# The combine stage of a mixture of experts: gate scaling on ScalarE and one VectorE add for five tiles

## The chip, the cores and the metric

The kernel runs on one core of one Trainium2 chip. The metric is the device time of one execution in microseconds (us); lower is better.

## What is computed

Two layers on 3125 nodes with 256 features. The first layer is a graph attention layer and a mixture of eight experts with the two best experts per node; the second is a plain graph sum and an attention over slices. The change lies between the two layers, where the experts' results are combined and the next layer norm and product are made:

```python
out = jnp.einsum('ne,nec->nc', gates, y)        # two gates per node are not zero
x = x + _L0_ffn_ref(...)                        # x += gate0 * y_first + gate1 * y_second
x = x + _L1_gnn_ref(_layernorm(x), L1_gnn_W, ...)  # starts with layernorm(x) @ W.T
```

## The kernel before, in words

The 3125 nodes are 25 tiles of 125 rows (`NT`), taken in 5 groups of 5 tiles (`GROUPS`, `TB`). The residual `k.res` stays in SBUF for the whole kernel. The stages are blocks with a barrier between them; the engines' programs are written out by hand, each engine works its own queue in that order, and semaphores join them. No planner moves anything.

`experts_phase` ends with the combine stage. Every result of an expert has been scattered to the DRAM table `y_tab`; SyncE waits for all of it (L1922 and around) and then loads, group by group, the first results and the second results of the five tiles into `ys`, which lies in the room of the expert weights (the trace calls it `weights`). Semaphores `ys_in[g]` and `seconds_in[g]` say that they have landed.

- **VectorE**, per group g: five `scalar_tensor_tensor` (L2188) make `res += gate0 * first`; then `invert(g-1)`, the reciprocal of the roots of the group before (L2182, waits for ScalarE's root); then five more (L2194) make `res += gate1 * second`, each raising `rows_made` by one; then five `bn_stats` (L2197) and four small operations (L2199 to L2202) for the variance, the last of which raises `deviations`.
- **TensorE**, per tile t: waits for `rows_made`, turns the tile into PSUM with two transposes (L2052), and then multiplies tile t-1 with the centred weight matrix (L2059, two products in float32). So the product of a group's last tile stands behind the transposes of the next group's first tile.
- **ScalarE**, per group: five copies of the turned tiles to SBUF (L2119), the square root of the variances (L2121), a wait for VectorE's reciprocal (`scaled`), and five scalings of the products by `rstd` into `xn` (L2125; the trace calls `xn` `e_x`), each waiting for its product.
- **SyncE** stores each scaled group to the DRAM table `xn_tab`. When all is stored the block ends, and `sum_phase` begins to gather rows of `xn_tab` with GpSimd (L1204).

The order on ScalarE that the change touches:

```python
for g in range(GROUPS):
    for t in tiles: ... nc.scalar.copy(yt[...], YT[...])        # L2119
    act.wait_ge(deviations, g + 1)
    nc.scalar.activation(k.rstd[...], spread[...], ACT.Sqrt, ...)   # L2121
    act.wait_ge(scaled, g + 1)
    for t in tiles: ... nc.scalar.activation(xn[:, t, :], XT[...], ACT.Identity, scale=k.rstd[...])  # L2125
```

Of the kernel before, what the change touches and what calls it, by code (L numbers as in the profile page):

```python
# [21 lines left out]
ALU = mybir.AluOpType  # L22
ACT = mybir.ActivationFunctionType
# [6 lines left out]
TB = 5  # L30
# [33 lines left out]
class Kernel:  # L64
# [10 lines left out]
    def sem(self, name):  # L75
        s = self.nc.semaphore(name)
        if self.opened is None:
            return self.ctx.enter_context(s)
        self.opened.append(self.layer.enter_context(s))
        return self.opened[-1]  # L80
# [973 lines left out]
class Prep:  # L1054
# [60 lines left out]
    def share(self, dve, t):  # L1115

        k = self.k
        k.steps["dve"](dve, k.nc.vector.scalar_tensor_tensor(out=k.res[:, t, :], in0=self.bias[:, :], scalar=self.part[:, t:t + 1], in1=k.res[:, t, :], op0=ALU.mult, op1=ALU.add))
# [745 lines left out]
def experts_phase(k):  # L1864
# [3 lines left out]
    nc = k.nc  # L1868
    ctx = ExitStack()
    X = XAHEAD  # L1870
    with ctx:
        sb = lambda n, s, d=F32: k.sb(f"e_{n}", s, d, ctx)
        sem = lambda n: k.sem(f"e_{n}")
# [12 lines left out]
        ys = k.weights[0:P, :, :].rearrange("p a w -> p (a w)")[:, 0:2 * NT * C].bitcast(F32).rearrange("p (j t c) -> p j t c", j=2, t=NT)  # L1886
        xn = x_more[0:P, 0:NT, :]
        GROUPS = NT // TB
# [3 lines left out]
        gw_mean, eps = sb("gw_mean", [128, 2]), sb("eps", [P, 1])  # L1892
        gap, spread = sb("gap", [P, NT]), sb("spread", [P, NT])
        gw_in, gw_centred, gw_turned, gw_ready = (sem(n) for n in ("gw_in", "gw_centred", "gw_turned", "gw_ready"))
        rows_made, y_turned, yt_kept, multiplied, xt_scaled = (sem(n) for n in ("rows_made", "y_turned", "yt_kept", "multiplied", "xt_scaled"))
        y_rows = k.y_tab.rearrange("(j t p) c -> p j t c", t=NT, p=P)
        deviations, roots, scaled, out_done = (sem(n) for n in ("deviations", "roots", "scaled", "out_done"))
        ys_in, seconds_in = [sem(f"ys_in{g}") for g in range(GROUPS)], [k.gather_sem(f"e_seconds_in{g}") for g in range(GROUPS)]
# [50 lines left out]
        def steps(start, item, finish):  # L1949


            start()
            for i in range(1, NI):
                item(i)
            finish()

        @block.tensor
        def _(pe):
# [86 lines left out]
            pe.wait_ge(y_kept, NI + 2)  # L2045
            for t in range(NT + 1):
                if t < NT:
                    pe.wait_ge(rows_made, t + 1)
                    if t >= XR:
                        pe.wait_ge(yt_kept, t - XR + 1)  # L2050
                    for c in range(2):
                        m = nc.tensor.transpose(YT[t % XR][:, c * P:(c + 1) * P], k.res[:, t, c * 128:(c + 1) * 128], k.ident[0:P, 0:P])  # L2052
                    m.then_inc(y_turned, 1)
                if t:
                    pe.wait_ge(yt_kept, t)
                    if t > len(XT):
                        pe.wait_ge(xt_scaled, t - len(XT))
                    for c in range(2):
                        m = nc.tensor.matmul(XT[(t - 1) % len(XT)], yt[:, (t - 1) % XR, c, :], gwt[:, c, :], start=(c == 0), stop=(c == 1))  # L2059
                    m.then_inc(multiplied, 1)  # L2060

        @block.scalar
        def _(act):
            act.sem_inc(y_kept, 2)

            def keep_x(i, s):
                act.wait_ge(x_turned, i + 1)
                act.wait_ge(up, 2 * i)
                nc.scalar.copy(xt[s][0][:, :, :].rearrange("p a m -> p (a m)"), TURN[:, 0:2 * M]).then_inc(x_high, 1)

            def silu(n, a):
                act.wait_ge(up, n + 3)
                act.wait_ge(h_made, n + 1)
                nc.scalar.activation(gated[a][:, 0:HH[a]], UP[a][:, 0:HH[a]], ACT.Silu).then_inc(silued, 1)  # L2074

            def keep_h(n, a):
                act.wait_ge(h_turned, n + 3)
                act.wait_ge(down, n + 1)
                nc.scalar.copy(ht[a][0][:, 0:2, :].rearrange("p b m -> p (b m)"), TH[:, 0:2 * M])
                nc.scalar.copy(ht[a][0][0:TAIL[a], 2, :], TH[0:TAIL[a], 2 * M:3 * M]).then_inc(h_high, 1)  # L2080

            def keep_y(i, s):
                act.wait_ge(down, 2 * i + 4)
                nc.scalar.copy(k.x_row(i), DOWN[s][:, 0:C]).then_inc(y_kept, 1)  # L2084

            def start():
                act.wait_ge(k.staged_in, 16)
                for raw, high, low in firsts:
                    nc.scalar.copy(high, raw).then_inc(first_high, 1)
                act.wait_ge(x_turned, 1)  # L2090
                nc.scalar.copy(xt[0][0][:, :, :].rearrange("p a m -> p (a m)"), TURN[:, 0:2 * M]).then_inc(x_high, 1)
                silu(0, 0)
                silu(1, 1)
                keep_x(1, 1)
                keep_h(0, 0)

            def item(i):
                silu(2 * i, 0)
                keep_h(2 * i - 1, 1)
                silu(2 * i + 1, 1)  # L2100
                if i < NI - 1:
                    keep_x(i + 1, (i + 1) % 2)
                keep_h(2 * i, 0)
                keep_y(i - 1, (i - 1) % 2)

            def finish():
                keep_h(2 * NI - 1, 1)
                keep_y(NI - 1, 1)

            steps(start, item, finish)  # L2110
            act.wait_ge(gw_turned, 1)
            nc.scalar.copy(gwt.rearrange("p a c -> p (a c)"), YT[0][:, 0:2 * C]).then_inc(gw_ready, 1)
            for g in range(GROUPS):
                tiles = range(g * TB, (g + 1) * TB)
                for t in tiles:
                    act.wait_ge(y_turned, t + 1)
                    if t >= XR:
                        act.wait_ge(multiplied, t - XR + 1)
                    nc.scalar.copy(yt[:, t % XR, :, :].rearrange("p a n -> p (a n)"), YT[t % XR][:, 0:2 * P]).then_inc(yt_kept, 1)  # L2119
                act.wait_ge(deviations, g + 1)  # L2120
                nc.scalar.activation(k.rstd[:, g * TB:(g + 1) * TB], spread[:, g * TB:(g + 1) * TB], ACT.Sqrt, bias=eps[:, 0:1], scale=1.0 / C).then_inc(roots, 1)  # L2121
                act.wait_ge(scaled, g + 1)
                for t in tiles:
                    act.wait_ge(multiplied, t + 1)
                    nc.scalar.activation(xn[:, t, :], XT[t % len(XT)], ACT.Identity, scale=k.rstd[:, t:t + 1]).then_inc(xt_scaled, 1)  # L2125

        @block.vector
        def _(dve):
            v = nc.vector
# [49 lines left out]
            def invert(g):  # L2179
                rstd = k.rstd[:, g * TB:(g + 1) * TB]  # L2180
                dve.wait_ge(roots, g + 1)
                v.reciprocal(rstd, rstd).then_inc(scaled, 1)  # L2182

            for g in range(GROUPS):
                tiles = slice(g * TB, (g + 1) * TB)
                dve.wait_ge(ys_in[g], 32)
                for t in range(g * TB, (g + 1) * TB):
                    m = v.scalar_tensor_tensor(out=k.res[:, t, :], in0=ys[:, 0, t, :], scalar=k.gate[:, 0, t:t + 1], in1=k.res[:, t, :], op0=ALU.mult, op1=ALU.add)  # L2188
                me(dve, m)
                if g:  # L2190
                    invert(g - 1)
                dve.wait_ge(seconds_in[g], 32)
                for t in range(g * TB, (g + 1) * TB):
                    v.scalar_tensor_tensor(out=k.res[:, t, :], in0=ys[:, 1, t, :], scalar=k.gate[:, 1, t:t + 1], in1=k.res[:, t, :], op0=ALU.mult, op1=ALU.add).then_inc(rows_made, 1)  # L2194
                dve.wait_ge(rows_made, (g + 1) * TB)
                for t in range(g * TB, (g + 1) * TB):
                    m = v.bn_stats(k.stats[:, t, :], k.res[:, t, :])  # L2197
                me(dve, m)
                v.tensor_tensor(spread[:, tiles], k.stats[:, tiles, 2], k.stats[:, tiles, 5], ALU.add)  # L2199
                me(dve, v.tensor_tensor(gap[:, tiles], k.stats[:, tiles, 1], k.stats[:, tiles, 4], ALU.subtract))  # L2200
                me(dve, v.scalar_tensor_tensor(out=gap[:, tiles], in0=gap[:, tiles], scalar=0.25 * C, in1=gap[:, tiles], op0=ALU.mult, op1=ALU.mult))
                v.tensor_tensor(spread[:, tiles], spread[:, tiles], gap[:, tiles], ALU.add).then_inc(deviations, 1)  # L2202
# [384 lines left out]
```

## Time and profile before

| | |
|---|---|
| median of 3 runs | 1933.1 us (1930.58 to 1934.11) |
| the profiled execution's own time | 1931.59 us |
| its span, first to last instruction | 1929.3 us |
| mean granted TensorE clock | 0.839 of full speed |
| TensorE, VectorE, ScalarE, GpSimd busy | 72%, 46%, 31%, 56% of the span |
| combine stage, first load issued to last product scaled | about 1180 to 1230 us |

Busy shares are means over stages with different limits. A timeline row gives start, length, engine, line, operation and, in brackets, how long the engine stood idle before it and what ended the wait. "x5" is five instructions merged into one row. PE is TensorE, DVE VectorE, ACT ScalarE, POOL GpSimd, SPq the queue of SyncE. [...]

### The profile page before, as it was taken

What the parts mean: (1) busy time and instruction counts of PE and PEld (TensorE: products, weight loads), DVE (VectorE), ACT (ScalarE), POOL (GpSimd) and SP (SyncE); (2) the same over time, 40 slices, a digit from 0 to 9 for tenths busy, and PEclk for the clock granted to TensorE, in tenths of its full rate; (3) what the DMA queues carried; (4) which work ended last, traced back from release to release, by engine and by line L of the source; (5) the groups of instructions that cost most, each with busy time, mean ns of one, the idle gap of its engine ahead of it and who ended that gap; (6) DMA issues with size and microseconds to landing.
All of it is one profiled execution on the core that took longest, in us unless ns stands there. A gap on an engine that the chain in (4) does not pass through costs nothing. (4 is left out here: it accounts for less than half of the span.)

```text
span 1929.3 us, 24683 instructions
## 1 busy us (share of the span) xinstructions
PE 1397.2 (72%) x7091; PEld 1166.9 (60%) x7091; DVE 878.9 (46%) x1858; ACT 594.9 (31%) x1305; POOL 1076.6 (56%) x1064
## 2 busy tenths in 40 slices
PE   6646666656665772899999996566666666668998
PEld 5535454445444762899999995444454444446787
DVE  6445544443444578333333334555333333336943
ACT  4144333333333233333333332322222222222310
POOL 1577777777773501783222570277777777763520
PEclk9857877877777685999999998787777888878999
DMA  6577989888886604432111125633333333330002
GB/s 164 129 226 249 301 282 307 269 275 295 287 277 207 147 1 124 147 87 92 46 47 47 44 93 106 178 104 104 106 105 104 106 105 105 106 88 1 0 1 67
DMA packets 156099, 266.53 MB, mean 138 GB/s; under 512 B 26388, under 2 KB 119331, under 8 KB 154953
## 3 DMA queue, kind: packets, MB, share of 16 engines
q1 hardware_dynamic: 106742, 138.90, 23.3%
q0 software_dynamic: 45424, 122.33, 21.0%
q10 hardware_dynamic: 3811, 3.78, 0.8%
q8 instruction: 64, 1.05, 0.2%
q14 instruction: 58, 0.48, 0.1%
HBM read 167.96 MB, written 97.93 MB: 138 GB/s over the span
## 5 line engine op out<-in xcount | busy, mean ns | idle before, releaser
L1204 POOL DMA_INDIRECT sum_rows<-xn_tab,src_e x391 | 373.2, 954 | 174.8 <-issue 118.8
L1229 PE MATMUL bank<-sum_held,sum_hot 128*125 128x256 f32 x976 | 309.3, 481 | 189.4 <-ACT sum_held L1239 188.1
L817 POOL DMA_INDIRECT gat_rows<-xh_tab,src_e x363 | 343.5, 946 | 114.7 <-issue 109.4
L1229 PEld LDWEIGHTS bank<-sum_held,sum_hot 128*125 128x125 f32 x976 | 225.3, 239 | 269.5 <-issue 175.1
L890 PE MATMUL bank<-gat_rows,gat_same 128*128 128x264 f32 x784 | 259.7, 477 | 126.1 <-issue 126.1
L890 PEld LDWEIGHTS bank<-gat_rows,gat_same 128*128 128x128 f32 x784 | 173.7, 240 | 165.2 <-issue 132.5
L1239 ACT COPY sum_held<-sum_rows 128x1024 f32 x122 | 127.5, 1045 | 373.3 <-SPq L1195 336.0
L1981 PE MATMUL bank<-weights,e_xthigh 128*128 x896 | 219.0, 328 | 10.0 <-DVE e_xtlow L2136 5.4
L934 ACT COPY gat_outs<-bank 128x528 f32<-128x528 f32 x196 | 117.3, 598 | 282.9 <-PE bank L890 282.4
L2141 DVE TENSOR_TENSOR e_h<-e_gated,bank 128x342 f32<-128x342 f32 x112 | 57.1, 510 | 263.5 <-ACT e_gated L2074 263.5
L1261 DVE SCALAR_TENSOR_TENSOR res<-bank,prep_inv,res 125x256 f32 x122 | 58.9, 483 | 235.0 <-PE bank L1229 228.0
L1981 PEld LDWEIGHTS bank<-weights,e_xthigh 128*128 128x128 f32 x896 | 152.6, 190 | 19.4 <-issue 19.3
L1981 PE MATMUL bank<-weights,e_xtlow 128*128 x448 | 143.9, 321 | 0.0
L2002 PE MATMUL bank<-weights,e_hthigh 128*128 (+2 forms) x672 | 134.6, 296 | 0.3 <-DVE e_htlow L2146 0.3
L2074 ACT ACTIVATE e_gated<-bank 128x342 f32<-128x342 f32 x112 | 51.0, 455 | 239.8 <-PE bank L1981 239.8
L1860 POOL CAST weights<-staged 128x4264 fp32r<-128x4264 f32 x7 | 26.3, 3751 | 151.9 <-SPq L1919 142.3
L854 DVE TENSOR_TENSOR gat_rows<-gat_rows,bank 128x1792 f32<-128x1792 f32 x56 | 110.3, 2009 | 0.8 <-ACT bank L926 0.8
L2002 PEld LDWEIGHTS bank<-weights,e_hthigh 128*128 128x128 f32 (+2 forms) x672 | 103.4, 191 | 0.5 <-issue 0.5
L2002 PE MATMUL bank<-weights,e_htlow 128*128 x336 | 94.4, 281 | 0.0
L1981 PEld LDWEIGHTS bank<-weights,e_xtlow 128*128 128x128 f32 x448 | 85.2, 190 | 0.0
L838 DVE TENSOR_TENSOR gat_logit<-gat_rows,adst_e 128x112 f32<-128x112 f32 x28 | 7.7, 277 | 164.2 <-DMA gat_rows<-xh_tab,src_e 164.2
L1946 POOL DMA_INDIRECT y_tab<-e_x,slot_row x52 | 50.9, 979 | 34.4 <-ACT e_x L2084 20.6
(537 smaller groups left out, 2500.5 us busy)
## 6 DMA issues: line engine op xcount, KB each, us to landing
parts<-gat_outs SPq DMA_DIRECT2D x27, 1904.0 KB, 8.0
staged<-w_tab SPq DMA_DIRECT2D x8, 2132.0 KB, 8.8
w_tab<-w_stage SPq DMA_DIRECT2D x16, 682.0 KB, 10.5
w_raw<-in_L_ffn_w_dram SPq DMA_DIRECT2D x16, 640.0 KB
gat_rows<-xh_tab,src_e POOLq DMA_INDIRECT x391, 4.6
sum_rows<-xn_tab,src_e POOLq DMA_INDIRECT x391, 2.8
w_tab<-w_stage SPq DMA_DIRECT2D x8, 768.0 KB, 10.6
weights<-y_tab SPq DMA_DIRECT2D x10, 600.0 KB
```

Of the source, the lines that this page charges most:

```text
L817: pool.indirect_dma_start(out=rows[b % R][:, t, :], out_offset=None, in_=k.xh_tab, in_offset=bass.IndirectOffsetOnAxis(ap=k.src_e[:, b * S ...
L854: v.tensor_tensor(f, f, weight[b % 2][:, t0 * H:t1 * H].rearrange("p (t h a) -> p t h a", h=H, a=1).to_broadcast([EP, SB // 2, H, D]), ALU ...
L890: m = nc.tensor.matmul(k.pairs[duo % DUOS][:, t % 2, 0:sums_w], same[b % 2][:, t, :], rows[b % R][:, t, 0:sums_w], start=True, stop=True)
L934: nc.scalar.copy(outs[b % 2][:, t:t + 2, 0:sums_w], k.pairs[duo % DUOS][:, :, 0:sums_w]).then_inc(taken, 1)
L1204: pool.indirect_dma_start(out=rows[:, at // IP % (RING * GPAIRS), at % IP, :], out_offset=None, in_=k.xn_tab, in_offset=bass.IndirectOffse ...
L1229: m = nc.tensor.matmul(k.ps[s][0:P, 0:C], hot[g % 2][:, s, c, :], held[:, s, c, :], start=(c == 0), stop=(c == IP - 1))
L1239: nc.scalar.copy(held_pair(n), pair).then_inc(staged, 1)
L1261: v.scalar_tensor_tensor(out=into, in0=k.ps[s][0:P, 0:C], scalar=prep.inv[:, bass.ds(node, 1)], in1=into, op0=ALU.mult, op1=ALU.add).then_ ...
L1981: last = nc.tensor.matmul(bank[:, 0:HH[a]], xt[s][px][:, c, :], part(slot, up_at(m, pw, c) + HB[a], 128, HH[a]), start=(n == 0), stop=(n = ...
L2002: m = nc.tensor.matmul(DOWN[s][:, 0:C], ht[a][ph][0:rows, b, :], part(slot, down_at(pw, 3 * a + b), rows, C), start=(a == 0 and n == 0), s ...
L2074: nc.scalar.activation(gated[a][:, 0:HH[a]], UP[a][:, 0:HH[a]], ACT.Silu).then_inc(silued, 1)
L2141: v.tensor_tensor(h[a][:, 0:HH[a]], gated[a][:, 0:HH[a]], GATE[a][:, 0:HH[a]], ALU.mult).then_inc(h_made, 1)
```

## The change

ScalarE gets a helper `share(g)`: it waits for the second results of group g and scales its five tiles by their gates from `ys` into `xn` (whose room is written again only later, by L2125). It is called once for group 0 ahead of the loop, and for group g+1 between the copies and the square root of group g. VectorE's five `scalar_tensor_tensor` per group become one `tensor_tensor` over 5 x 256 columns, which waits for the five scaled tiles; `rows_made` now counts groups, and TensorE waits for the whole group ahead of its first tile.

```diff
-                    pe.wait_ge(rows_made, t + 1)
+                    pe.wait_ge(rows_made, t // TB + 1)
...
+            def share(g):
+                act.wait_ge(seconds_in[g], 32)
+                for t in range(g * TB, (g + 1) * TB):
+                    nc.scalar.activation(xn[:, t, :], ys[:, 1, t, :], ACT.Identity, scale=k.gate[:, 1, t:t + 1]).then_inc(shared, 1)
+
+            share(0)
             for g in range(GROUPS):
...
                     nc.scalar.copy(yt[:, t % XR, :, :].rearrange("p a n -> p (a n)"), YT[t % XR][:, 0:2 * P]).then_inc(yt_kept, 1)
+                if g < GROUPS - 1:
+                    share(g + 1)
                 act.wait_ge(deviations, g + 1)
...
-                dve.wait_ge(seconds_in[g], 32)
-                for t in range(g * TB, (g + 1) * TB):
-                    v.scalar_tensor_tensor(out=k.res[:, t, :], in0=ys[:, 1, t, :], scalar=k.gate[:, 1, t:t + 1], in1=k.res[:, t, :], op0=ALU.mult, op1=ALU.add).then_inc(rows_made, 1)
-                dve.wait_ge(rows_made, (g + 1) * TB)
+                dve.wait_ge(shared, (g + 1) * TB)
+                v.tensor_tensor(k.res[:, tiles, :], xn[:, tiles, :], k.res[:, tiles, :], ALU.add).then_inc(rows_made, 1)
+                dve.wait_ge(rows_made, g + 1)
```

## Rows read from the trace of the kernel before

**Rows 1.** Windows; columns: us, busy and count per engine, PEclk, DMA, GB/s.
```profile
1190.00:1197.00 7.00, 6.20 (x19) 4.76 (x20) 6.35 (x19) 1.47 (x4) 0.00 (x0) 0.53 1.07 197
1214.00:1221.00 7.00, 5.89 (x30) 4.55 (x30) 6.48 (x21) 3.93 (x12) 0.00 (x0) 1.00 0.75 238
```

**Rows 2.** Timeline of VectorE, from one reciprocal to the next.
```profile
1213.67 0.19 DVE L2182 RECIPROCAL rstd<-rstd 125x5 f32<-125x5 f32 x1 [0.38 <-ACT rstd L2121]
1213.77 2.03 DVE L2194 SCALAR_TENSOR_TENSOR res<-weights,gate,res 125x256 f32<-125x256 f32 x5
...
1220.60 0.19 DVE L2182 RECIPROCAL rstd<-rstd 125x5 f32<-125x5 f32 x1 [0.38 <-ACT rstd L2121]
```

**Rows 3.** Timeline of ScalarE, same stretch.
```profile
1213.89 1.57 ACT L2125 ACTIVATE e_x<-bank,rstd 125x256 f32<-125x256 f32 x4 [0.32 <-DVE rstd L2182]
...
1215.98 0.63 ACT L2119 COPY staged<-bank 128x250 f32<-128x250 f32 x2
...
1219.94 0.37 ACT L2119 COPY staged<-bank 128x250 f32<-128x250 f32 x1 [0.71 <-PE bank L2052]
1220.20 0.30 ACT L2121 ACTIVATE rstd<-e_spread,e_eps 125x5 f32<-125x5 f32 x1
```

**Rows 4.** Timeline of TensorE, same stretch.
```profile
1214.27 0.43 PE L2052 MATMUL bank<-ident,res 125*128 125x125 f32 x2 [0.44 <-DVE res L2194]
...
1217.36 0.38 PE L2052 MATMUL bank<-ident,res 125*128 125x125 f32 x2
...
1218.44 0.38 PE L2052 MATMUL bank<-ident,res 125*128 125x125 f32 x2
...
1221.21 0.44 PE L2052 MATMUL bank<-ident,res 125*128 125x125 f32 x2 [0.44 <-DVE res L2194]
```

**Rows 5.** Timeline, the start of the stage's first group.
```profile
1190.12 2.07 DVE L2194 SCALAR_TENSOR_TENSOR res<-weights,gate,res 125x256 f32<-125x256 f32 x5 [1.42 <-DMA weights<-y_tab]
...
1190.76 1.07 PE L2052 MATMUL bank<-ident,res 125*128 125x125 f32 x4 [13.15 <-DVE res L2194]
...
1193.73 0.62 PE L2052 MATMUL bank<-ident,res 125*128 125x125 f32 x2
...
1195.85 0.62 PE L2052 MATMUL bank<-ident,res 125*128 125x125 f32 x2
```

**Rows 6.** Groups by line and shape, whole kernel; columns: busy us, mean ns, idle before.
```profile
L1587 DVE TENSOR_TENSOR join_main<-join_main,join_wt 125x1280 f32<-125x1280 f32 x5 | 7.5, 1492 | 0.2
...
L1730 ACT ACTIVATE r_xn<-res,r_shift,rstd 125x256 f32<-125x256 f32 x25 | 12.4, 586 | 0.0
...
L2112 ACT COPY staged<-bank 128x512 f32<-128x512 f32 x1 | 0.6, 585 | 0.3 <-PE bank L2042 0.3
...
L2399 ACT ACTIVATE t_logit<-t_logit 125x512 f32<-125x512 f32 x25 | 15.9, 636 | 2.7 <-POOL t_logit L2262 2.7
```

**Rows 7.** Timeline, the end of the stage.
```profile
1227.70 1.93 ACT L2125 ACTIVATE e_x<-bank,rstd 125x256 f32<-125x256 f32 x5 [0.26 <-DVE rstd L2182]
...
1230.01 0.40 SPq L140 DMA_DIRECT2D xn_tab<-e_x  x1
...
1235.08 1.00 POOL L1204 DMA_INDIRECT sum_rows<-xn_tab,src_e  x1 [55.94 <-POOLq L1871]
```

**Rows 8.** Timeline of TensorE in the next stage, two bursts after a wait.
```profile
1308.73 3.25 PE L1229 MATMUL bank<-sum_held,sum_hot 128*125 128x256 f32 x8 [2.74 <-ACT sum_held L1239]
...
1318.91 7.12 PE L1229 MATMUL bank<-sum_held,sum_hot 128*125 128x256 f32 x24 [3.22 <-ACT sum_held L1239]
```

**Rows 9.** Windows around those two bursts; columns as in Rows 1.
```profile
1309.00:1312.00 3.00, 2.99 (x8) 1.84 (x6) 1.36 (x2) 0.00 (x0) 2.27 (x3) 0.54 0.38 113
...
1319.00:1320.00 1.00, 1.00 (x4) 0.85 (x5) 0.00 (x0) 1.00 (x1) 0.69 (x2) 0.74 0.44 131
1320.00:1322.00 2.00, 2.00 (x6) 1.54 (x6) 0.00 (x0) 0.00 (x0) 1.70 (x2) 0.50 0.44 121
1322.00:1323.00 1.00, 1.00 (x4) 0.82 (x3) 0.67 (x2) 0.12 (x1) 0.69 (x2) 0.55 0.26 78
```

More of the change, by code:

```diff
@@ L1894, in experts_phase @@
         gw_in, gw_centred, gw_turned, gw_ready = (sem(n) for n in ("gw_in", "gw_centred", "gw_turned", "gw_ready"))
-        rows_made, y_turned, yt_kept, multiplied, xt_scaled = (sem(n) for n in ("rows_made", "y_turned", "yt_kept", "multiplied", "xt_scaled"))
+        rows_made, y_turned, yt_kept, multiplied, xt_scaled, shared = (sem(n) for n in ("rows_made", "y_turned", "yt_kept", "multiplied", "xt_scaled", "shared"))
         y_rows = k.y_tab.rearrange("(j t p) c -> p j t c", t=NT, p=P)
```

## The prediction

> **What bounds the kernel now.** I read the windows first, to see where in the span the change lies and which engines are full there, then one timeline of a single group on three engines, and last the start and the end of the stage. In a window of the combine stage VectorE is busy 6.48 of 7.00 us, TensorE 5.89 and ScalarE 3.93 [rows 1]. The obvious reading is that VectorE is nearly full and ScalarE has room for five more operations. The timeline says otherwise. A group takes from one reciprocal to the next, 1213.67 to 1220.60, 6.93 us, and each time VectorE has waited for ScalarE's square root just before its reciprocal [rows 2]. The root itself starts right behind the group's fifth copy (1219.94, then 1220.20), and that copy had waited for TensorE's transposes [rows 3]. The transposes follow each other every 1.08 us (1217.36 to 1218.44), and the burst opens 0.50 us after VectorE's first L2194 starts (1213.77 to 1214.27) [rows 2, 4]. So the group's cycle is a ring: reciprocal, first gated add, TensorE's five tiles, fifth copy, root, reciprocal. Only what lies in that ring sets the time. ScalarE's idle time lies inside the ring, ahead of its copies, and is of no use to an instruction queued behind the last copy. Nothing after the stage takes a delay back: the last products are scaled from 1227.70 on, the last store is issued at 1230.01, and GpSimd, idle for 55.94 us, starts the next stage's gathers at 1235.08 [rows 7].
>
> **What it adds, in the ring.** Three things get longer.
>
> *The price of one gate scaling on ScalarE.* The trace has no activation of 125x256 from SBUF with one pointer operand. Below it lies L2125, the same with a PSUM source: four take 1.57 us and five 1.93, so one more costs 0.36 [rows 3, 7]. Above it lies L1730, SBUF to SBUF with two pointer operands: 12.4 us for 25, 0.50 each [rows 6]. An SBUF source without pointers costs 0.05 more than a PSUM copy of the same 512 columns (636 against 585 ns) [rows 6]. I take 0.36 + 0.05 = 0.41, the row that differs in the source alone plus that difference. One alone then lasts 1.57 - 3 x 0.36 + 0.05 = 0.54, and five 4 x 0.41 + 0.54 = 2.18 us.
>
> [...]
>
> *The start.* Before, L2194 starts at 1190.12 when the second results land, and TensorE at 1190.76 [rows 5]. After, ScalarE starts at that landing and takes 2.18; then VectorE adds the five tiles in one operation. Its price is L1587's, the same operation on 125x1280: 1.49 us [rows 6]. TensorE, which now waits for the whole group, started 0.50 after the first add when warm; it will start about 1.51 after the big one does. So the start is late by 2.18 + 1.51 - 0.50 = 3.2 us.
>
> *The four later groups.* Behind the same reciprocal the five adds take 2.03 [rows 2] and the one 1.49, so VectorE saves 0.54 a group. But TensorE could start after the first of five and must now wait for the one: 1.51 against 0.50, 1.01 us later. That is 4 x 1.01 = 4.0 us. The fifth scaling of the group before waits for a product queued behind those transposes, so it is late by the same step, not by more.
>
> *The shares in the loop.* Group g+1's five scalings sit between the fifth copy and the root of group g, four times: 4 x 5 x 0.41 = 8.2 us. The root's own input has been ready long before, so the whole of it is added. The new wait there, for the second results of the next group, costs nothing: at 1213.77 L2194 found them landed [rows 2], and ScalarE asks for the same ones only after the copies of the group before, which the terms above move to about 1222. If a load were late there, the root, the five scalings and the next copies behind it would all be late with it.
>
> Free are: VectorE's new wait for `shared` (the scalings precede the root that releases the reciprocal ahead of it), the five statistics (they end long before the root is due), and the stores, which follow the last scaling and come late by the same sum. SyncE's loads are queued ahead of its stores as before, GpSimd has nothing in this stage. Up to here: 3.2 + 4.0 + 8.2 = 15.4 us.
>
> *The clock.* This is the term that the instruction list doesn't show. Between two bursts TensorE now stands idle for 0.44 us [rows 4]; with 1.01 and 5 x 0.41 added it will be 3.5 us, four times. In the next stage, bursts after a wait of 2.74 and 3.22 us run into a lower level: the mean granted clock is 0.54 in the three us from 1309, and after 1318.91 it goes 0.74, 0.50, 0.55 [rows 8, 9]. [...] At that level a tile takes 2.12 us (1193.73 to 1195.85) instead of 1.08 [rows 4, 5], so 3.4 us at the low level cost 1.7 us of work. Some of it falls where TensorE waits for ScalarE's copies anyway; I take 1.6, four times, 6.4 us. The lower bound is nothing, if the clock holds. The upper is a burst like the first group's, which started cold: a mean of 0.53 over 1190 to 1197 [rows 1, 5] puts the rise at 1196.6, 5.8 us after its start, 2.9 us of work lost; 4 x 2.9 = 11.6.
>
> **The sum** is 15.4 + 6.4 = 21.8 us. Against the profiled execution's own 1931.59 (its span of 1929.3 and 2.3 around it) that gives 1953.4; the median of the runs shown, 1933.1, is 1.5 above that execution and gives 1954.9. I forecast 1955.
>
> **The rivals.**
> - *The clock holds* in the longer waits. For it: in this stage it reads 1.00 throughout a warm window [rows 1], and a wait falls nearer to 3.3 us if the scalings cost 0.36. Against it: 2.74 us was enough elsewhere [rows 8, 9]. It gives 15.4 alone, 1947 to 1949. Chance 0.13.
> - *Whole bursts run at the low level*, because a burst this short is over before the clock rises. Each burst then loses 5 x 1.04 = 5.2 us: 15.4 + 20.8 = 36.2, 1968 to 1969. For it: the first group needed 5.8 us; against it: 3.4 us sufficed at 1319. Chance 0.08.
> - *Not slower: VectorE is the bound*. Place: VectorE's queue between two reciprocals, 6.48 busy in 7.00 [rows 1], 0.38 idle. If that queue set the cycle, and ScalarE's scalings ran in its waits before the copies, the 0.54 saved would come off five times, -2.7 us, 1930.4. It decides if the root is ready before VectorE comes to the reciprocal; every row of a reciprocal shows VectorE waiting for it [rows 2], and the added scalings stand ahead of that root in a queue worked in order. Chance 0.03.
> - *The change doesn't do what it says*: another table load on ScalarE for these activations, 25 small ones and no gain. L2125 is the same function and ran behind the root with nothing in between [rows 3, 7], so I give it no time and 0.02 for this and all else.
>
> **How the numbers follow.** The forecast's own case has 0.74. Its bounds: scalings of 0.36 or 0.50 move the sum by -1.2 or +2.1; the clock's term by -6.4 or +5.2. The low end takes in the holding clock with cheap scalings: 1954.9 - 6.4 - 1.2 = 1947.3, and 1945.8 from the profiled execution's own time: 1946. The high end takes the forecast with cold bursts like the first group's and a little of the dear scalings: 1954.9 + 5.2 + 0.9 = 1961. Left out are the rival of whole cold bursts, the not-slower one and the rest, 0.13. A measurement of this kernel tells about 0.2%, 3.9 us, from no change. Of the cases only the third lies within that, so slower has 0.95, no change 0.04 and faster 0.01.
>
> **What would show it.** In the profile after: five activations from `weights` into `e_x` between the fifth copy and each of the first four roots, 2.0 to 2.2 us together; one add of 1.49 us; the first transposes at 3.2 us after their old distance from the landing; reciprocals 10 to 12 us apart instead of 6.93, the last gap about 8 to 10; waits of some 3.5 us ahead of L2052; a granted clock that falls to 0.50 once per group. Wrong would be: reciprocals under 8 us apart, scalings that overlap the copies' waits, or a next stage that starts at its old time. If the clock stays at 1.00 in the stage, the first rival holds; if it stays at 0.50, the second.

## The result, and the profile after

The changed kernel takes 1957.09 us (median of 4 runs, 1955.07 to 1959.39) against 1933.61 of the kernel before in the same comparison: ratio 1.0129, 95% interval 1.0114 to 1.0144, 23.5 us slower. The forecast was 1955.

The profiled execution of after took 1959.39 us. Where the time lies is seen best by the stage alone, from ScalarE's last copy of an expert's result to the first gather of the next stage. The two timelines give 58.06 us before and 81.58 after, 23.5 more; so all of the difference lies here (the experts' stage ahead of it ended 4.3 us later in this one execution). First the row of before that opens the stage (it ends at 1235.08, [rows 7]):

```profile
1177.02 0.37 ACT L2084 COPY e_x<-bank 128x256 f32<-128x256 f32 x1 [2.24 <-PE bank L2002]
```

then the two of after:

```profile
1181.31 0.37 ACT L2084 COPY e_x<-bank 128x256 f32<-128x256 f32 x1 [2.24 <-PE bank L2002]
...
1262.89 1.00 POOL L1204 DMA_INDIRECT sum_rows<-xn_tab,src_e  x1 [79.46 <-POOLq L1871]
```

The timeline of VectorE after, the counterpart of [rows 2]:

```profile
1209.29 0.19 DVE L2190 RECIPROCAL rstd<-rstd 125x5 f32<-125x5 f32 x1 [6.64 <-ACT rstd L2129]
1209.40 1.45 DVE L2201 TENSOR_TENSOR res<-e_x,res 125x1280 f32<-125x1280 f32 x1
...
1222.02 0.19 DVE L2190 RECIPROCAL rstd<-rstd 125x5 f32<-125x5 f32 x1 [6.75 <-ACT rstd L2129]
...
1233.15 0.19 DVE L2190 RECIPROCAL rstd<-rstd 125x5 f32<-125x5 f32 x1 [5.15 <-ACT rstd L2129]
...
1245.90 0.19 DVE L2190 RECIPROCAL rstd<-rstd 125x5 f32<-125x5 f32 x1 [6.77 <-ACT rstd L2129]
...
1255.29 0.19 DVE L2190 RECIPROCAL rstd<-rstd 125x5 f32<-125x5 f32 x1 [5.07 <-ACT rstd L2129]
```

The distances are 12.73, 11.13, 12.75 and 9.39 us instead of four times 6.9. VectorE's work is shorter (1.45 for the add), and what it gained it spends waiting for the root, 5 to 7 us a group instead of 0.38. The timeline of ScalarE after, the end of a group (compare [rows 3]), shows what stands ahead of the root now:

```profile
1194.53 2.10 ACT L2116 ACTIVATE e_x<-weights,gate 125x256 f32<-125x256 f32 x5 [12.02 <-DMA weights<-y_tab]
...
1219.37 0.37 ACT L2125 COPY staged<-bank 128x250 f32<-128x250 f32 x1 [0.71 <-PE bank L2052]
1219.63 2.10 ACT L2116 ACTIVATE e_x<-weights,gate 125x256 f32<-125x256 f32 x5
1221.64 0.28 ACT L2129 ACTIVATE rstd<-e_spread,e_eps 125x5 f32<-125x5 f32 x1
```

The timeline of TensorE after: the first transposes of the five bursts, with the waits ahead of them in brackets (compare [rows 4, 5]):

```profile
1198.38 1.07 PE L2052 MATMUL bank<-ident,res 125*128 125x125 f32 x4 [16.48 <-DVE res L2201]
...
1210.90 0.68 PE L2052 MATMUL bank<-ident,res 125*128 125x125 f32 x2 [4.86 <-DVE res L2201]
...
1223.63 0.43 PE L2052 MATMUL bank<-ident,res 125*128 125x125 f32 x2 [3.44 <-DVE res L2201]
...
1234.76 0.68 PE L2052 MATMUL bank<-ident,res 125*128 125x125 f32 x2 [3.44 <-DVE res L2201]
...
1247.83 0.43 PE L2052 MATMUL bank<-ident,res 125*128 125x125 f32 x2 [3.76 <-DVE res L2201]
```

The windows of after over groups 1 to 4, two to a group (columns as in [rows 1]; PEclk is the third entry from the end):

```profile
1210.00:1216.00 6.00, 4.69 (x13) 3.33 (x14) 5.13 (x15) 2.08 (x6) 0.00 (x0) 0.57 1.07 204
1216.00:1222.00 6.00, 4.20 (x19) 3.23 (x17) 0.00 (x0) 3.29 (x9) 0.00 (x0) 0.86 0.56 164
1223.00:1227.00 4.00, 2.96 (x10) 2.13 (x11) 3.86 (x13) 1.81 (x6) 0.00 (x0) 0.68 0.07 19
1227.00:1233.00 6.00, 4.32 (x21) 3.19 (x20) 1.00 (x3) 3.24 (x9) 0.00 (x0) 0.93 0.36 94
1234.00:1240.00 6.00, 4.83 (x13) 3.49 (x14) 4.99 (x15) 1.94 (x6) 0.00 (x0) 0.56 0.23 49
1240.00:1246.00 6.00, 4.07 (x19) 3.09 (x17) 0.10 (x1) 3.29 (x9) 0.00 (x0) 0.87 0.20 61
1247.00:1251.00 4.00, 2.76 (x9) 1.96 (x10) 3.09 (x10) 1.69 (x5) 0.00 (x0) 0.67 0.00 0
1251.00:1256.00 5.00, 5.00 (x25) 4.19 (x25) 0.19 (x1) 1.79 (x6) 0.00 (x0) 0.92 0.49 128
```

PEclk, the clock granted to TensorE as a share of full speed, was 1.00 throughout a group before [rows 1]; now it falls in each of the four bursts. Taken in windows of 1 us it reads 0.50 in all six from 1211 to 1217 (group 1) and in both from 1249 to 1251 (group 4).

### The profile page after: what moved, and what is told of

The parts are those of the page before. It is cut to its first block and busy times, and to the rows that moved or that the text cites. A ratio compares the mean times of both kernels' runs of the same rounds, so it can differ in the third digit from the quotient of the medians.

```text
span 1957.4 us, 24689 instructions
## 1 busy us (share of the span) xinstructions
PE 1406.4 (72%) x7091; PEld 1174.0 (60%) x7091; DVE 875.1 (45%) x1838; ACT 604.7 (31%) x1330; POOL 1075.1 (55%) x1064
## 5 line engine op out<-in xcount | busy, mean ns | idle before, releaser
L1247 DVE TENSOR_TENSOR sum_hot<-bank,walk_local 128x2000 f32<-128x2000 f32 x31 | 69.0, 2226 | 2.6 <-DMA prep_bias<-in_L_gnn_b_dram 2.6
```

Of the source, the lines that this page charges most:

```text
L1247: v.tensor_tensor(hot[g % 2][:, :, :, :], lane.rearrange("p (a b n) -> p a b n", a=1, b=1).to_broadcast([EP, IB, IP, P]), w.local[:, g * I ...
```

## The experiments

Ratios are to the kernel before, with 95% intervals. "Distances" are those between the five reciprocals, "stage" the length from ScalarE's last copy of an expert's result to the first gather, as above; both come from the one profiled execution of each run.

**1 and 2: hold the clock.** TensorE multiplies the unit matrix while it waits; the second run has 13 products instead of 18.

```diff
-                    pe.wait_ge(rows_made, t // TB + 1)
                     if t >= XR:
                         pe.wait_ge(yt_kept, t - XR + 1)
+                    if t and t % TB == 0:
+                        for _ in range(18):
+                            nc.tensor.matmul(YT[t % XR][:, 256:384], k.ident[:, :], k.ident[:, :], start=True, stop=True)
+                    pe.wait_ge(rows_made, t // TB + 1)
```

> The changed kernel with 18 extra small matmuls on TensorE ahead of its wait for each of groups 1 to 4; their product is used by nobody. Theory (the ring got longer by scalings, the late add and, on top, a clock that falls in the longer wait): the waits fill up, the granted clock stays at 1.00 from group 1 on, the reciprocals come 10.0 us apart (6.93 + 1.01 + 2.05) instead of 11.1 to 12.8, and some 8 us of the 23.5 come back: about 1949, ratio to the kernel before 1.008. Rival (the clock is only a witness, the products wait for ScalarE anyway): reciprocals stay 11 to 13 us apart, 1957, ratio 1.012 to 1.013, or more, as the extra matmuls are in the way.

Measured: 1.0077 [1.0052, 1.0102], distances 9.93, 10.29, 10.29, 8.24. The first distance is the one forecast; in the next two the 18 products, 4.0 us from the first to the transposes behind them, outlasted the wait.

> The changed kernel with 13 extra small matmuls per wait instead of 18, which had taken 4.0 us of a 3.5 us wait and so delayed groups 2 to 4 by 0.36 each. Theory: the clock still holds at 1.00, all four distances are 9.9, 9.9, 9.9 and 7.9 us, the stage is 73.4 us long; the clock's share of the change is then 81.6 - 73.4 = 8.2 us; 1948, ratio 1.0075. Rival (only matmuls that fill the whole wait hold the clock): it falls in some groups and distances of 11 to 12.7 return.

Measured: 1.0072 [1.0054, 1.009], distances 9.93, 9.94, 9.93, 8.19, stage 73.04 us (1174.52 to 1247.56). Windows of this run over groups 1 and 2:

```profile
1203.00:1213.00 10.00, 8.79 (x56) 7.60 (x56) 5.91 (x17) 5.93 (x18) 0.00 (x0) 1.00 0.92 206
1213.00:1223.00 10.00, 8.79 (x56) 7.61 (x56) 5.90 (x17) 5.93 (x17) 0.00 (x0) 1.00 0.29 79
```

PEclk reads 1.00 throughout, and in groups 3 and 4 as well. The work is that of after with the unused products in TensorE's waits, and what differs is the clock: the four distances are 8.0 us shorter together than those of after. The stage is 81.58 - 73.04 = 8.5 us shorter, but the other 0.5 lie ahead of the first reciprocal, where no unused product stands; there the first burst, which in every run starts at PEclk 0.50 after a wait of 13.2 to 16.5 us, took 6.42 us from its first transposes to the fifth copy against 6.83 after. The clock is a cause, not a witness, and with 8.0 of 23.5 us a third of the loss.

**3: the same work in another place.** The scalings go between the copies (`share` takes a range of tiles here).

```diff
                     nc.scalar.copy(yt[...], YT[...]).then_inc(yt_kept, 1)
-                if g < GROUPS - 1:
-                    share(g + 1)
+                    if g < GROUPS - 1 and 1 <= t % TB <= 3:
+                        share(g + 1, *((0, 2), (2, 4), (4, 5))[t % TB - 1])
```

> The changed kernel with the five scalings of the next group placed between the copies (two behind the second copy, two behind the third, one behind the fourth) instead of behind the fifth. Theory: the same work on ScalarE now falls into its waits for transposes; 8.0 us leave the ring, TensorE's wait between bursts shrinks to about 1.5 us, so the clock holds and gives back 8 more: reciprocals about 8.0 us apart, left are the late start (3.2) and the late add (4.0), perhaps 1.5 where group 0 asks early for group 1's second results: about 1941 to 1943, ratio 1.004. Rival (it is the amount of work on ScalarE that costs, wherever it stands): the copies are delayed by the scalings one for one and the time stays at 1955 to 1957.

Measured: 1.0035 [1.0024, 1.0046], distances 9.61, 7.94, 7.94, 8.19. The distances from group 2 on are as forecast; the first is not, as TensorE's wait ahead of group 1 was 2.86 us and not 1.5, and the clock fell in that burst (PEclk 0.72 over 1204 to 1210, with 0.50 from 1207.0 to 1209.5):

```profile
1204.41 0.44 PE L2052 MATMUL bank<-ident,res 125*128 125x125 f32 x2 [2.86 <-DVE res L2201]
```

ScalarE of this run, with the root now right behind the fifth copy:

```profile
1217.52 0.37 ACT L2125 COPY staged<-bank 128x250 f32<-128x250 f32 x1 [0.36 <-PE bank L2052]
1217.78 0.91 ACT L2116 ACTIVATE e_x<-weights,gate 125x256 f32<-125x256 f32 x2
1218.60 0.37 ACT L2125 COPY staged<-bank 128x250 f32<-128x250 f32 x1
1218.86 0.51 ACT L2116 ACTIVATE e_x<-weights,gate 125x256 f32<-125x256 f32 x1
1219.68 0.37 ACT L2125 COPY staged<-bank 128x250 f32<-128x250 f32 x1 [0.31 <-PE bank L2052]
1219.94 0.30 ACT L2129 ACTIVATE rstd<-e_spread,e_eps 125x5 f32<-125x5 f32 x1
```

The copies stand 1.08 us apart (1217.52, 1218.60, 1219.68), TensorE's own pace: the scalings are free here. Experiment 2, at the same clock, had 9.93 with them behind the fifth copy, 2.0 a group more. 7.94 is 6.93 + 1.01, the late add alone.

**4 and 5: each part alone.** First the scalings without their user: the kernel before, with `share(g + 1)` behind the fifth copy.

> The kernel before with the five scalings of the next group behind the fifth copy, four times; VectorE still does its own gated adds and nobody uses the scaled tiles. Theory: 4 x 2.05 = 8.2 us in the ring, and TensorE's wait grows to 2.5 us, near where the clock falls elsewhere: with a clock that falls in some of the groups 2 to 6 more, 1944 to 1948, ratio 1.005 to 1.0075. Rival (VectorE's wait for the scalings, not ScalarE's queue, is the cost): 1934, ratio 1.000.

Measured: 1.0068 [1.0044, 1.0092], stage 70.22 us (1176.02 to 1246.24, 12.2 more), distances 10.12, 10.12, 10.13, 8.07. TensorE's wait is 3.86 us ahead of group 1 and 2.44 ahead of the three later groups, and the clock falls in each of the four (the wait ahead of group 2, then windows over its burst and the rest of the group):

```profile
1210.92 0.43 PE L2052 MATMUL bank<-ident,res 125*128 125x125 f32 x2 [2.44 <-DVE res L2201]
...
1211.00:1215.00 4.00, 3.60 (x12) 2.53 (x13) 3.86 (x14) 2.11 (x7) 0.00 (x0) 0.57 0.64 206
1215.00:1221.00 6.00, 3.61 (x20) 2.74 (x18) 2.44 (x8) 3.63 (x10) 0.00 (x0) 1.00 0.33 96
```

Then the one add without the scalings:

```diff
-                    pe.wait_ge(rows_made, t + 1)
+                    pe.wait_ge(rows_made, t // TB + 1)
...
-                for t in range(g * TB, (g + 1) * TB):
-                    v.scalar_tensor_tensor(... scalar=k.gate[:, 1, t:t + 1] ...).then_inc(rows_made, 1)
+                v.tensor_tensor(k.res[:, tiles, :], ys[:, 1, tiles, :], k.res[:, tiles, :], ALU.add).then_inc(rows_made, 1)
...
```

> The kernel before with one add of five tiles in place of the five gated adds; the second gates are left out of the sum and ScalarE does nothing new. Theory: TensorE starts 1.01 us later in each of five groups, 5.0 us; its wait is 1.5 us and the clock holds: 1938 to 1939, ratio 1.0026. Rival (VectorE's 0.54 saved per group counts): 1931, ratio 0.999.

Measured: 1.0034 [1.002, 1.0047], stage 64.01 us (1181.54 to 1245.55, 6.0 more), distances 9.16, 7.94, 7.94, 8.19. The distances at the high clock are as forecast, the first is not. In the kernel before TensorE's wait ahead of group 1 is 1.86 us and not 0.44, because a table load of 1.28 stands between the fifth copy and ScalarE's first root. The clock stayed at 1.00 behind that wait (1200 to 1207):

```profile
1200.40 0.43 PE L2052 MATMUL bank<-ident,res 125*128 125x125 f32 x2 [1.86 <-DVE res L2194]
```

With 1.01 more it became 2.86, and the clock fell (that wait, then windows over group 1 and over group 2):

```profile
1206.34 0.43 PE L2052 MATMUL bank<-ident,res 125*128 125x125 f32 x2 [2.86 <-DVE res L2193]
...
1206.00:1215.00 9.00, 7.26 (x30) 5.44 (x30) 5.69 (x17) 3.72 (x12) 0.00 (x0) 0.81 1.07 201
1215.00:1223.00 8.00, 5.88 (x30) 4.54 (x30) 5.90 (x17) 3.94 (x12) 0.00 (x0) 1.00 0.85 229
```

The parts alone cost 12.2 and 6.0; with the five scalings at the start, 2.2, that is 20.4 of the 23.5. Of the other 3, 2.0 are the clock's: it costs 8.0 in the four bursts of after, 1.2 in each of the four of experiment 4 and 1.2 in one of experiment 5. The rest, 1.1, is of the size by which the first burst varies: it took 6.25 us in experiment 4 and 6.19 in experiment 5 against 6.83 after and 6.96 before. The clock rose from 0.50 to 1.00 at another moment of it: 4.4 us after the first transposes in experiment 4 and 4.3 in experiment 5, against 5.6 after and 5.8 before.

**6: the change without its two lengthenings.** Experiment 3, and the add made tile by tile, each waiting for its own scaled tile and releasing TensorE for it.

("The second run" is experiment 3 here.)

> The changed kernel with the scalings between the copies, as in the second run, and the add made tile by tile again (each waits for its own scaled tile and releases TensorE for it). Theory: with both lengthenings out of the ring the reciprocals are 6.9 us apart again and the clock holds; left are some 0.5 us at the start and up to 1.5 where ScalarE asks for group 1's second results inside group 0: 1934 to 1937, ratio 1.000 to 1.001. No gain, though VectorE does less per tile (0.41 against 0.48 us a tile): VectorE is not in the ring. Rival (moving the multiplication off VectorE is worth its saved time once nothing is in its way): 2 us or more under the kernel before, ratio 0.999.

Measured: 1.0014 [1.0004, 1.0024], distances 6.88, 6.87, 6.87, 6.81. VectorE of this run:

```profile
1208.85 1.72 DVE L2202 TENSOR_TENSOR res<-e_x,res 125x256 f32<-125x256 f32 x5
...
1215.62 0.19 DVE L2190 RECIPROCAL rstd<-rstd 125x5 f32<-125x5 f32 x1 [0.62 <-ACT rstd L2129]
```

Five adds take 1.72 instead of 2.03, and VectorE waits 0.62 instead of 0.38: most of the relief turns into waiting, and the four distances are 0.2 us shorter together, not four times 0.31. The stage is 1.9 us longer than before (59.92, 1177.01 to 1236.93), and all of that lies ahead of the first reciprocal, as forecast: TensorE starts 0.6 later (14.31 after the stage's start instead of 13.74), and the other 1.5 come where ScalarE asks for the second results of group 1 inside group 0 and stands waiting for them:

```profile
1197.20 0.91 ACT L2116 ACTIVATE e_x<-weights,gate 125x256 f32<-125x256 f32 x2 [4.41 <-DMA weights<-y_tab]
```

**7 and 8: shorten the ring itself.** In the kernel before, each scaling by `rstd` moves behind a copy of the next group (`scale(t)` holds the lines removed below, with both waits).

```diff
                     nc.scalar.copy(yt[...], YT[...]).then_inc(yt_kept, 1)
+                    if g:
+                        scale(t - TB)
...
-                act.wait_ge(scaled, g + 1)
-                for t in tiles:
-                    act.wait_ge(multiplied, t + 1)
-                    nc.scalar.activation(xn[:, t, :], XT[...], ACT.Identity, scale=k.rstd[:, t:t + 1]).then_inc(xt_scaled, 1)
+            for t in range(NT - TB, NT):
+                scale(t)
```

> The kernel before with one edit of ScalarE's order alone: the scaling of a tile of the group before stands behind each copy of the next group, instead of all five ahead of the copies. Theory of the ring: TensorE's product of the first tile no longer waits 0.6 us for a copy behind the scalings, the root comes some 0.9 us earlier, and VectorE's own work (about 6.5 us a group) becomes the bound: distances of 6.5 instead of 6.93, 1.5 to 2 us less, ratio 0.999. Rival (the loads, one group in 7.0 us, pace the stage): VectorE then waits for loads and the time is 1933.6.

Measured: 0.9985 [0.9974, 0.9997], distances 6.59, 6.59, 6.58, 6.52. VectorE of this run:

```profile
1213.82 2.06 DVE L2193 SCALAR_TENSOR_TENSOR res<-weights,gate,res 125x256 f32<-125x256 f32 x5
1215.92 0.19 DVE L2187 RECIPROCAL rstd<-rstd 125x5 f32<-125x5 f32 x1
```

No wait stands ahead of the reciprocal: only now is VectorE the bound. The stage takes 56.76 us (1179.79 to 1236.55), 1.3 less than before, and the whole time lies just under that of before, by an interval that ends at 0.9997.

> The run before with one more edit: a square root of one column, used by nobody, ahead of the loop, while ScalarE waits for the loads, so that the table load of 1.28 us is out of the first group. Theory: the load stood in the ring (copy, table load, root, reciprocal), so 1.3 us more come off, some 3 us in all against the kernel before, ratio 0.9985. Rival (the first group waits for its successor's loads anyway): nothing beyond the run before.

Measured: 0.9984 [0.9972, 0.9996]; the stage is 55.57 us (1175.09 to 1230.66) against 56.76 of the run before, though in the whole time the two can't be told apart. From the fifth copy of group 0 to its root it is 0.27 us (1195.80 to 1196.07) instead of 1.69 (1200.65 to 1202.34), so the load is out of the ring. One of the distances is 6.97, the others 6.5 to 6.6: ahead of it VectorE waits 0.25 us for second results.

**9: relieve VectorE where it is the bound.**

Experiments 6 and 7 in one kernel ("the sixth-run order" is that of experiment 6).

> The sixth-run order (scalings of the second results between the copies, tile-wise add) together with the order in which the scalings by rstd also stand between the copies. There VectorE had no wait left ahead of its reciprocal and set the cycle with 6.59 us a group. Theory: with VectorE in the ring its saved time counts at last: five adds take 1.72 instead of 2.03 us, distances of 6.3 us, 1 us off the stage against the order alone, some 0.5 us back at the start: 1930 to 1932, ratio 0.998 to 0.999. Rival (ScalarE, which now has copies, both scalings and a root to do in 6.3 us, and asks for second results earlier than VectorE did, becomes the next bound, or the loads do): distances of 6.6 to 7.0, 1933 to 1936, ratio 1.000 to 1.001.

Measured: 1.0025 [1.0015, 1.0036], distances 7.01, 7.01, 7.01, 6.47: the rival, in both of its parts. Timelines of ScalarE and VectorE of this run, first from group 0, then from group 2:

```profile
1197.34 0.91 ACT L2116 ACTIVATE e_x<-weights,gate 125x256 f32<-125x256 f32 x2 [4.54 <-DMA weights<-y_tab]
...
1213.17 0.92 ACT L2116 ACTIVATE e_x<-weights,gate 125x256 f32<-125x256 f32 x2
1213.96 0.38 ACT L2130 COPY staged<-bank 128x250 f32<-128x250 f32 x1
1214.21 0.50 ACT L2122 ACTIVATE e_x<-bank,rstd 125x256 f32<-125x256 f32 x1
1214.58 0.53 ACT L2116 ACTIVATE e_x<-weights,gate 125x256 f32<-125x256 f32 x1
1214.98 0.39 ACT L2130 COPY staged<-bank 128x250 f32<-128x250 f32 x1
1215.23 0.52 ACT L2122 ACTIVATE e_x<-bank,rstd 125x256 f32<-125x256 f32 x1
1215.60 0.34 ACT L2136 ACTIVATE rstd<-e_spread,e_eps 125x5 f32<-125x5 f32 x1
...
1216.03 0.19 DVE L2195 RECIPROCAL rstd<-rstd 125x5 f32<-125x5 f32 x1 [0.76 <-ACT rstd L2136]
```

ScalarE has no wait left from the third copy to the root, and VectorE waits for it again: in groups 1 to 4 it is ScalarE, not the loads, as no wait for a load is left there. In group 0 it is a load, the 4.54 us for the second results of group 1. Against experiment 7 the stage is 3.5 us longer (60.22, 1176.83 to 1237.05); 2.2 of that lie ahead of the first reciprocal (0.7 by TensorE's later start, the rest by that wait) and 1.2 in the four distances.

## Why the prediction was right, and where a term was off

- **The ring** held. At the high clock the scalings cost 2.0 us a group behind the fifth copy and nothing between the copies (distances of 9.93 in experiment 2, 7.94 in experiment 3), so it is their place, not their amount, as long as ScalarE has waits left there (in experiment 9 it has not).
- **One scaling**: 0.41 forecast. From the first of five to the root is 2.01 us (1219.63 to 1221.64), 0.40 each, so 8.0 instead of 8.2.
- **The late add**: 1.01 a group forecast, 7.94 - 6.93 = 1.01 measured (experiments 3 and 5). Only the last group has more, 8.19 - 6.87 = 1.32: there the add starts 0.38 after the reciprocal and not 0.11.
- **The start**: 3.2 forecast. TensorE starts 3.85 after ScalarE's first scaling (1194.53 to 1198.38), against 0.64 after the landing before [rows 5]: 3.21.
- **The loads, the stores and VectorE's new wait** cost nothing in the loop, as said: after ScalarE's first scaling no engine of the stage waits for a load in after.
- **The clock** was the mis-sized term, in the step that let each burst lose 1.6 us. No run shows the 1.6; it was the author's estimate. What the runs show in its place: the distances of after exceed those of experiment 2 by 2.80, 1.19, 2.82 and 1.20, 8.0 together instead of 6.4. The rows behind the step, a low stretch of 3.4 us in the next stage, fit two bursts only: from 1319 PEclk is 0.74, 0.50 and 0.55 over 1, 2 and 1 us [rows 9], and shared out between the two levels 1.00 and 0.50 that makes 0.52 + 2 + 0.9 us at 0.50. The windows of after, shared out in the same way, give 3.4 us at 0.50 for group 2 (4 x 0.64 + 6 x 0.14) and as much for group 4, but 6.8 for group 1 (6 x 0.86 + 6 x 0.28) and for group 3. So two bursts lost 1.2 more than the step said and two lost 0.4 less; that the sum of the four came as near as 1.6 us is partly luck.
- **The waits** ahead of the bursts were forecast at 3.5 us, all four; they are 4.86, 3.44, 3.44 and 3.76. The 0.44 us of [rows 4] that the step started from holds for three of them, while ahead of group 1 the wait was 1.86 before, for the table load.
- **The sum** was 21.8, the stage grew by 23.5: 8.0 by the clock's fall in the four bursts (6.4 forecast) and 15.5 by all else (15.4 forecast).

Of the rivals, the holding clock would have given 1947 to 1949; experiment 2, where it does hold, has 1.0072, some 1947.5. That VectorE was the bound is excluded by its waits of 5 to 7 us for the root after, and by experiment 6, where five of its adds are 0.3 us shorter and the cycle is only 0.06. What is not settled is why the low level lasted twice as long in two of the four bursts. The wait ahead of a burst does not decide it: two waits of 3.44 us were followed by 3.4 us (group 2) and 6.8 us (group 3) at PEclk 0.50. The rows show only that in groups 1 and 3 the clock is low as the burst opens (first transposes 0.68 us), and that in groups 2 and 4 it is still high then (0.43) and falls within the burst. No run varied a burst alone.

## What to carry to other kernels

Before work moves to an idle engine, find the wait that closes the cycle and see on which side of it the new instructions land in that engine's queue: here the same five scalings cost 2.0 us a group behind the last copy and nothing between the copies. Ask too what the new place makes the engine wait for: between the copies of group 0 the scalings stood waiting 4.41 us for a load (experiment 6). One big add in place of five gated ones took less time here, 1.45 us instead of 2.03, and released TensorE 1.01 us later; where the reader consumes tile by tile, the first release counts. And price what a longer wait does to TensorE afterwards: behind waits of 3.44 to 4.86 us PEclk fell to 0.50 for 3.4 to 6.8 us, and that was 8.0 of the 23.5 us lost.

## What was not expected of the hardware

- The clock fell to PEclk 0.50 after waits of 2.44 us ahead of three groups of experiment 4, and of 2.86 in experiments 3 and 5, while 1.86 left it at 1.00 in the kernel before. Experiment 5 makes every wait 1.0 us longer: where that led from 1.86 to 2.86 the clock fell, and where it led from 0.44 to 1.45 it held at 1.00 (1215 to 1223).
- The table load costs about what its row shows, 1.28 us: with it, the fifth copy and the root stand 1.69 us apart in experiment 7, without it 0.27 in experiment 8, 1.42 less. In after no wait stands on either side of it: the scalings ahead of the load end at 1207.57 and it starts at 1207.60, it ends at 1208.88 and the root starts at 1208.89.

```profile
1205.47 2.10 ACT L2116 ACTIVATE e_x<-weights,gate 125x256 f32<-125x256 f32 x5
1207.60 1.28 ACT L2129 ACT_TABLE_LOAD   x1
1208.89 0.30 ACT L2129 ACTIVATE rstd<-e_spread,e_eps 125x5 f32<-125x5 f32 x1
```
